# Edge pass of a graph network: operands of the one-hots and values moved to a PSUM bank, and an order of its own for TensorE

## The chip, the cores and the metric

The kernel runs on one core of a Trainium2 chip. The metric is the device time of one execution in microseconds, as the median of several executions. The engines are named as the profile names them: PE is TensorE (PEld is its weight load), DVE is VectorE, ACT is ScalarE, POOL is GpSimd and SP is SyncE.

## The reference, cut to what matters

A two-layer graph attention network over 6250 nodes and 100000 edges, followed by a feed-forward block on half of the rows. Everything that the change touches is the attention over edges, done once in each of the two layers:

```
src = concatenate([src0, arange(n)])        # self edges are added
dst = concatenate([dst0, arange(n)])        # dst0 comes sorted
q, k, v = ...reshape(n, 8, 32)              # 8 heads of 32
scores = einsum('ehd,ehd->eh', q[dst], k[src]) * scale
m   = segment_max(scores, dst)
ex  = exp(scores - m[dst])
z   = segment_sum(ex, dst)
agg = segment_sum((ex / z[dst])[:, :, None] * v[src], dst)
```

The two layers differ in weights only. Before, between and after them come dense stages over the nodes (projections, a merge of partial sums, normalisations, the feed-forward blocks), which the change leaves as they are.

## The kernel before, in words

`edge_pass` does the attention over edges of one layer. The sorted edges are cut into 832 steps of at most 128 edges with one block of 128 destination nodes each; eight steps are a group (`G = 8`), worked as four pairs (`PAIRS`, numbered `m` from 0 to 3). There are 104 groups in a pass. `groups_of` runs the first four and the last four groups as straight code and the others in a loop whose body holds four groups. A group's number modulo 4 is its lane; the buffers of rows `kv` have four lanes.

Five engines run one program each, tied by three counters (`dve_p`, `act_p`, `pe_p`: semaphores on which an engine ticks named steps, and on which the others wait for a step of a given group).

For each step, POOL gathers the key and value rows of the source nodes, 128 rows of 512 numbers, by an indirect DMA (L673) whose row numbers lie in the tile `idx` in SBUF. It waits until PE has ended its sums over the group that used the same lane four groups earlier. SP loads the small tables and the edges' offsets ahead.

DVE makes a one-hot matrix `spread` for a whole group from the offsets (L697). PE multiplies it with the block's queries, which gives each edge its query (`spread_q`, L805, step `q{m}`, two banks of PSUM, so two pairs ahead). DVE multiplies keys and queries (`product`, L715) and sums over each head (`score`, L722). When all four pairs of a group are done, PE transposes the scores into PSUM (`turn`, L834, step `score_t`), DVE takes the running maximum in both directions along the edges (`up`, L737, and `top`, L744), and PE transposes the maxima back (L842, step `max_t`). DVE subtracts them from the scores (`below`, L749) and keeps the maxima with the rows (`maxima`, L750), and ACT takes the exponential, which gives the weights (step `weights`, L909), into the columns `KV:KV + H` of `kv` in SBUF.

For each pair DVE then compares the column numbers 0 to 127 (`keep["cols"]`, a constant in SBUF) with each edge's node column (`tab`, SBUF), which gives a one-hot matrix (`sel`, L758), and multiplies the values by the weights in place (`value`, L764). PE multiplies the one-hots with the weighted values and adds into one of four PSUM banks (L852, steps `sums{j}`, two per pair); after two pairs it makes the sums of the rows at the ends of the steps (L863, steps `ends0` and `ends1`). ACT copies each step's sum bank to the accumulator `acc` (L919) and sets a bank that is done with to zero by copying a tile of zeros (L920, step `acc{j}`). PE's sums of a pair wait for ACT's `acc` of the step before it.

Both transposes share one bank of PSUM, `turned`: the scores turned are its first 128 columns on 64 partitions (`pst`), the maxima turned back are the 64 columns after them (`psm`).

The work of neighbouring groups is interleaved by a list, `WEAVE`, that DVE and PE both run through for each group; ACT has its own list, `ACT_WEAVE`. `product`, `score` and `turn` belong to the group itself. `up`, `top`, `weigh` (below and maxima) and `tail` (sel, value, sums of pairs 0 and 1) belong to the group before it, and `late` (the same of pairs 2 and 3) to the group two before it. An engine runs its instructions in the order of its program, so a wait holds up all that stands behind it. On PE `product m` stands for the `spread_q` two pairs ahead, that is of pair `m + 2` of the group or of pair `m - 2` of the next one.

Of the kernel before, what the change touches and what calls it, by code (L numbers as in the profile page):

```python
# [16 lines left out]
ALU = mybir.AluOpType  # L17
ACT = mybir.ActivationFunctionType
# [5 lines left out]
P = 128  # L24
N, D = 6250, 256
E = 100000
H, DH = 8, 32
# [3 lines left out]
SCALE = DH ** -0.5  # L31
# [13 lines left out]
G = 8  # L45
# [10 lines left out]
KV = 2 * D  # L56
# [93 lines left out]
def bc(ap, shape):  # L150

    return ap.broadcast_to(shape)
# [271 lines left out]
def constants(nc, keep):  # L424

    with Phase(nc) as ctx:
# [17 lines left out]
        def _(dve):  # L444
# [8 lines left out]

WEAVE = (("product", 0), ("late", 2), ("score", 0), ("up", 0), ("product", 1), ("top", 0), ("late", 3),
         ("score", 1), ("weigh", 0), ("product", 2), ("tail", 0), ("score", 2), ("product", 3), ("tail", 1),
         ("score", 3), ("turn", 0))
ACT_WEAVE = (("late", 2), ("weigh", 0), ("late", 3), ("tail", 0), ("tail", 1))
PAIRS = G // 2
# [5 lines left out]
def later(turn, n):  # L464

    lane, k, c = turn
    g = 4 * c + lane + n
    return (g % 4, k, g // 4)
# [5 lines left out]

CLEARED = 3

# [10 lines left out]
def edge_pass(nc, layer, dram, keep):  # L487

    with Phase(nc) as ctx:
# [3 lines left out]
        def ps(name, shape, dt=F32):  # L493
            return ctx.enter_context(nc.psum_tensor(f"edge{layer}_{name}", shape, dt))
# [5 lines left out]
        kv = sb("kv", [P, LANES, G, ROW])  # L500
# [11 lines left out]
        sel = sb("sel", [P, G, P])  # L512
        score = sb("score", [P, 2, G * H])
        up = sb("up", [G * H, P])
# [4 lines left out]
        pst = turned[0:G * H, 0:P]  # L519
        psm = turned[:, P:P + G * H]  # L520
        psa = ps("sums", [P, SUMS * BANKED])
        pse = ps("end_sums", [P, 512])
# [13 lines left out]
        for m in range(PAIRS):  # L536
            dve_steps += [f"product{m}", f"score{m}"]
        dve_steps += ["up", "top", "below", "maxima"]
        for m in range(PAIRS):
            dve_steps += [f"sel{m}", f"value{m}"]  # L540
        dve_p.begin(dve_steps)
        pe_p.begin([f"q{m}" for m in range(PAIRS)] + ["score_t", "max_t"] 
                   + [f"sums{j}" for j in range(HALF)] + ["ends0"] + [f"sums{j}" for j in range(HALF, G)] + ["ends1"])
# [142 lines left out]
        def _(dve):  # L686
            v = nc.vector
            v.memset(zeros[:, :], 0.0).then_inc(s_clear, 1)
            v.memset(blank[:, :], 0.0).then_inc(s_clear, 1)
            v.memset(pse[:, :], 0.0).then_inc(s_clear, 1)  # L690
            dve.wait_ge(s_clear, CLEARED)

# [38 lines left out]
            def scan_up(turn):  # L731
# [6 lines left out]
                           turn, "up")  # L738

            def rest(turn, what, m, earliest=False):  # L740
                lane = turn[0] % 2
                if what == "top":
                    dve_p.wait(dve, turn, "up")
                    dve_p.tick(v.tensor_tensor_scan(top[:, ::-1], flags[:, lane, 1, ::-1], up[:, ::-1], -BIG,  # L744
                                                    ALU.add, ALU.max), turn, "top")
                elif what == "weigh":
                    table(turn)
                    pe_p.wait(dve, turn, "max_t")
                    dve_p.tick(v.tensor_tensor(below[:, :], score[:, lane, :], psm, ALU.subtract), turn, "below")  # L749
                    dve_p.tick(v.tensor_tensor(kv[:, turn[0], :, KV + H:ROW], psm.rearrange("p (j h) -> p j h", h=H),  # L750
                                               bc(tab[:, turn[0], :, 1:2], [P, G, H]), ALU.mult),
                               turn, "maxima")
                elif what in ("tail", "late"):

                    if not earliest:
                        pe_p.wait(dve, later(turn, -1), f"sums{2 * m + 1}")
                    at = 2 * m
                    dve_p.tick(v.tensor_tensor(sel[:, at:at + 2, :], bc(keep["cols"][:, :].unsqueeze(1), [P, 2, P]),  # L758
                                               bc(tab[:, turn[0], 2 * m:2 * m + 2, 0:1], [P, 2, P]),
                                               ALU.is_equal), turn, f"sel{m}")  # L760
                    if m == 0:
                        act_p.wait(dve, turn, "weights")
                    values = kv[:, turn[0], 2 * m:2 * m + 2, D:KV].rearrange("p j (h d) -> p j h d", h=H)
                    dve_p.tick(v.tensor_tensor(values, values,  # L764
                                               bc(kv[:, turn[0], 2 * m:2 * m + 2, KV:KV + H].unsqueeze(3), [P, 2, H, DH]),
                                               ALU.mult), turn, f"value{m}")

            spread_of((0, None, 0), True)
            groups_of(dve, body)
            rest(later(LAST_TURN, -1), "late", 2)  # L770
            scan_up(LAST_TURN)
            rest(LAST_TURN, "top", 0)
# [6 lines left out]
        def _(pe):  # L779
# [36 lines left out]
            def body(turn, begun=4, end=False):  # L816
                places = {}
                for what, m in WEAVE:

# [60 lines left out]
        def _(act):  # L880
# [20 lines left out]
            def rest(turn, what, m, places, earliest=False):  # L901
                lane = turn[0] % 2
                if what == "weigh":
# [4 lines left out]
                    dve_p.wait(act, turn, "below")  # L908
                    act_p.tick(s.activation(kv[:, turn[0], :, KV:KV + H], below[:, :].rearrange("p (j h) -> p j h", h=H),  # L909
                                            ACT.Exp, scale=SCALE), turn, "weights")  # L910
                elif what in ("tail", "late"):
# [1550 lines left out]
```

## Time and profile before

| | us |
|---|---|
| median of 3 runs | 4388.59 (4388.18 to 4395.11) |
| the profiled execution, its time | 4386.98 |
| its span from the first to the last instruction | 4385.3 |
| busy: PE, DVE, ACT, POOL over the span | 3657.6, 3202.1, 1681.7, 2061.5 |

The time of the profiled execution is what the chip reported for it, and the span is what its trace shows between the first and the last instruction. In a row of a group of instructions, `x` is the count, then come busy microseconds and the mean nanoseconds of one, then the time that the engine sat idle just before them and what ended it (`<-`). "issue" is time in which the engine waited for nothing that the trace shows. In a row of the timeline the first two numbers are the start and the duration in microseconds, and the idle time just before stands in brackets.

### The profile page before, as it was taken

The page shows a single profiled execution, that of the slowest core. Times are in us where ns is not written, and L with a number is a line of the kernel's source. Part 1 is how long each engine was busy: PE and PEld are TensorE (multiplying, and loading weights), DVE is VectorE, ACT ScalarE, POOL GpSimd, SP SyncE. Part 2 cuts the span into 40 slices and gives each one's busy share as a digit, 9 for nine tenths or more (in the row PEclk, how much of TensorE's full clock was granted, in tenths as well). Part 3 has the DMA queues.
Part 4 walks back from the last instruction along what each step waited for, and adds up shares of the span by engine and source line. Part 5 has one row for each costly group of instructions (what it writes and reads, how often), then busy time and mean ns, then how long its engine had stood idle before and what let it go on. Part 6 is the DMA issues. An engine that isn't in the chain of part 4 may idle for free. (4 is left out here: it accounts for less than half of the span.)

```text
span 4385.3 us, 82262 instructions
## 1 busy us (share of the span) xinstructions
PE 3657.6 (83%) x17048; PEld 2421.9 (55%) x17048; DVE 3202.1 (73%) x7179; ACT 1681.7 (38%) x4755; POOL 2061.5 (47%) x1914
## 2 busy tenths in 40 slices
PE   1998889888898848999978898888889668888488
PEld 0654555555555427777755555555555337777377
DVE  4888999898989865555558898988899656666501
ACT  0114555555555502222225555555555302222022
POOL 2117777777777610000037777777777400000012
PEclk8999999999999979999989999999999879999699
DMA  3337777777777511111137777777777502222011
GB/s 72 120 112 220 217 217 220 212 216 211 215 215 218 173 62 48 48 60 60 48 118 211 214 219 211 218 213 209 212 219 220 165 22 75 84 78 78 26 46 39
DMA packets 357833, 640.42 MB, mean 146 GB/s; under 512 B 107755, under 2 KB 199981, under 8 KB 357594
## 3 DMA queue, kind: packets, MB, share of 16 engines
q0 software_dynamic: 140144, 457.44, 35.3%
q1 hardware_dynamic: 217610, 182.03, 14.1%
q8 instruction: 36, 0.59, 0.1%
q14 instruction: 43, 0.35, 0.0%
HBM read 570.14 MB, written 69.95 MB: 146 GB/s over the span
## 5 line engine op out<-in xcount | busy, mean ns | idle before, releaser
L673 POOL DMA_INDIRECT edge_kv<-kv,edge_idx x1664 | 1868.8, 1123 | 541.4 <-issue 416.9
L852 PE MATMUL edge_sums<-edge_kv,edge_sel 128*128 128x272 f32 x3328 | 982.9, 418 | 141.3 <-ACT edge_sums L920 111.8
L805 PE MATMUL edge_q<-qc,edge_spread 128*128 x3328 | 921.1, 400 | 153.1 <-DVE edge_kv L715 128.8
L919 ACT COPY acc<-edge_sums x1664 | 641.2, 385 | 869.5 <-PE edge_sums L852 699.2
L805 PEld LDWEIGHTS edge_q<-qc,edge_spread 128*128 128x128 f32 x3328 | 578.5, 191 | 431.6 <-issue 377.0
L852 PEld LDWEIGHTS edge_sums<-edge_kv,edge_sel 128*128 128x128 f32 x3328 | 567.5, 190 | 440.9 <-issue 363.1
L715 DVE TENSOR_TENSOR edge_kv<-edge_kv,edge_q 128x512 f32<-128x512 f32 x832 | 565.6, 680 | 242.9 <-DMA edge_kv<-kv,edge_idx 229.6
L920 ACT COPY edge_sums<-edge_blank 128x272 f32 x1664 | 659.7, 396 | 0.0
L764 DVE TENSOR_TENSOR edge_kv<-edge_kv 128x512 f32<-128x512 f32 x832 | 565.0, 679 | 0.8 <-ACT edge_kv L909 0.8
L722 DVE TENSOR_REDUCE edge_score<-edge_kv 128x16 f32<-128x512 f32 x832 | 560.0, 673 | 0.2
L758 DVE TENSOR_TENSOR edge_sel<-cols,edge_tab 128x256 f32<-128x256 f32 x832 | 340.3, 409 | 0.0
L1440 POOL TENSOR_TENSOR middle_rs<-middle_var,middle_power 128x2 f32<-128x2 f32 x50 | 34.7, 693 | 571.9 <-DVE middle_minus_half L1464 571.9
L863 PE MATMUL edge_end_sums<-edge_kv,edge_tab 128*2 128x272 f32 x3328 | 268.2, 394 | 0.0
L1440 POOL TENSOR_TENSOR last_rs<-last_var,last_power 128x2 f32<-128x2 f32 x50 | 34.7, 694 | 479.9 <-DVE last_minus_half L1464 479.9
L1627 PE MATMUL middle_ph<-middle_xt,middle_w 128*128 128x256 f32 x800 | 185.6, 386 | 28.5 <-ACT middle_xt L1705 28.5
L1627 PE MATMUL last_ph<-last_xt,last_w 128*128 128x256 f32 x800 | 181.7, 386 | 27.8 <-ACT last_xt L1705 27.8
L1627 PEld LDWEIGHTS last_ph<-last_xt,last_w 128*128 128x128 f32 x800 | 151.6, 192 | 53.9 <-ACT last_xt L1705 33.9
L1627 PEld LDWEIGHTS middle_ph<-middle_xt,middle_w 128*128 128x128 f32 x800 | 149.7, 192 | 53.4 <-ACT middle_xt L1705 20.4
L1637 PE MATMUL last_pp<-last_w,last_hid 128*128 128x256 f32 x800 | 176.7, 379 | 0.0
L1637 PE MATMUL middle_pp<-middle_w,middle_hid 128*128 128x256 f32 x800 | 176.7, 379 | 0.0
L697 DVE TENSOR_SCALAR edge_spread<-edge_rel,part 128x1024 f32<-128x1024 bf16 x208 | 160.3, 771 | 6.2 <-DMA edge_rel<-step_rel 6.2
L1637 PEld LDWEIGHTS last_pp<-last_w,last_hid 128*128 128x128 f32 x800 | 152.0, 190 | 20.7
(369 smaller groups left out, 3912.1 us busy)
## 6 DMA issues: line engine op xcount, KB each, us to landing
edge_rel<-step_rel SPq DMA_DIRECT2D x208, 256.0 KB
edge_kv<-kv,edge_idx POOLq DMA_INDIRECT x1664, 3.9
edge_flags<-step_flags SPq DMA_DIRECT2D x416, 32.0 KB
picked<-last_picked SPq DMA_DIRECT2D x25, 513.0 KB
kv<-first_kv_out SPq DMA_DIRECT2D x25, 512.0 KB
kv<-middle_kv_out SPq DMA_DIRECT2D x25, 512.0 KB
end_rows<-edge_ends SPq DMA_DIRECT2D x416, 8.5 KB
h<-first_h SPq DMA_DIRECT2D x25, 256.0 KB
```

The costliest lines, as they stand in the source:

```text
L673: nc.gpsimd.indirect_dma_start(kv[:, turn[0], j, 0:KV], None, dram["kv"], bass.IndirectOffsetOnAxis(ap=idx[:, turn[0], j:j + 1], axis=0)). ...
L715: dve_p.tick(v.tensor_tensor(k_rows, k_rows, psq[m % QBUFS][:, :, :], ALU.mult), turn, f"product{m}")
L722: dve_p.tick(v.tensor_reduce(score[:, lane, 2 * m * H:2 * (m + 1) * H].rearrange("p (j h) -> p j h", h=H), k_rows.rearrange("p j (h d) -> ...
L758: dve_p.tick(v.tensor_tensor(sel[:, at:at + 2, :], bc(keep["cols"][:, :].unsqueeze(1), [P, 2, P]), bc(tab[:, turn[0], 2 * m:2 * m + 2, 0:1 ...
L764: dve_p.tick(v.tensor_tensor(values, values, bc(kv[:, turn[0], 2 * m:2 * m + 2, KV:KV + H].unsqueeze(3), [P, 2, H, DH]), ALU.mult), turn, ...
L805: mm = t.matmul(psq[m % QBUFS][:, j % 2, :], spread[:, turn[0] % 2, j * P:(j + 1) * P], qc[:, bass.ds(at[j % 2], D)], start=True, stop=True)
L852: pe_p.tick(t.matmul(psa[:, bass.ds(place[j % 2], QC)], sel[:, j, :], kv[:, turn[0], j, D:ROW], start=False, stop=True, skip_group_check=T ...
L863: mm = t.matmul(pse[32 * q:32 * q + 2, 0:QC], tab[:, turn[0], j, 2:4], kv[:, turn[0], j, D:ROW], start=True, stop=True)
L919: s.copy(acc[:, bass.ds(at, QC)], psa[:, bass.ds(bank, QC)])
L920: act_p.tick(s.copy(psa[:, bass.ds(spent, QC)], blank[:, :]), turn, f"acc{j}")
L1627: mm = t.matmul(ph[bank // 2][:, at:at + W * P], mat[:, half, c * P:(c + 1) * P], xt[:, i, half * W * P:(half + 1) * W * P], start=(half = ...
L1637: mm = t.matmul(pp[turn[0]][:, w * D:(w + 1) * D], hid[:, turn[0], at:at + P], mat[:, c, :], start=(c == 0), stop=(c == FF // P - 1))
```

## The change

The column numbers are copied once per pass into the last 128 columns of the bank `turned` (`cols`), and `sel` reads them from there. The exponential is taken twice by ACT: into 64 more columns of that bank (`psw`), from which `value` now reads the weights, and as before into `kv`, with which PE sums them. `below` comes after `maxima`. DVE waits for the step `max_t` of the next group ahead of `late` 3 (`follows`), and for the weights ahead of the `sel` of pair 0, no longer between it and its `value`. `up` and `top` keep their place after `score` 0 and `product` 1 on DVE, while `late` 2 moves behind `up`, `late` 3 behind `product` 2, `weigh` behind `late` 3, and `tail` 0 behind `product` 3. PE gets its own list, `PE_WEAVE`, in which the transposes stand ahead of sums that they followed before: `max_t` directly behind `late` 2 and ahead of the `spread_q` of `product` 1, and the transpose of the scores ahead of the sums of `tail` 1. `late` 3 comes after the `spread_q` of `product` 2.

```diff
@@ -451,9 +451,11 @@
 
 
 
-WEAVE = (("product", 0), ("late", 2), ("score", 0), ("up", 0), ("product", 1), ("top", 0), ("late", 3),
-         ("score", 1), ("weigh", 0), ("product", 2), ("tail", 0), ("score", 2), ("product", 3), ("tail", 1),
+WEAVE = (("product", 0), ("score", 0), ("up", 0), ("late", 2), ("product", 1), ("top", 0), ("score", 1),
+         ("product", 2), ("late", 3), ("weigh", 0), ("score", 2), ("product", 3), ("tail", 0), ("tail", 1),
          ("score", 3), ("turn", 0))
+PE_WEAVE = (("product", 0), ("late", 2), ("top", 0), ("product", 1), ("product", 2), ("late", 3), ("product", 3),
+            ("tail", 0), ("turn", 0), ("tail", 1))
 ACT_WEAVE = (("late", 2), ("weigh", 0), ("late", 3), ("tail", 0), ("tail", 1))
 PAIRS = G // 2
 QBUFS = 2
@@ -472,7 +474,7 @@
     return turn[1] is None and turn[0] == 0 and turn[2] == 0
 
 
-CLEARED = 3
+CLEARED = 4
 
 
 def values_of(nc, engine, ap, most):
@@ -518,6 +520,8 @@
         turned = ps("turned", [P, 512])
         pst = turned[0:G * H, 0:P]
         psm = turned[:, P:P + G * H]
+        psw = turned[:, P + G * H:P + 2 * G * H].rearrange("p (j h) -> p j h", h=H)
+        cols = turned[:, 512 - P:512]
         psa = ps("sums", [P, SUMS * BANKED])
         pse = ps("end_sums", [P, 512])
 
@@ -535,11 +539,11 @@
         dve_steps = ["spread"]
         for m in range(PAIRS):
             dve_steps += [f"product{m}", f"score{m}"]
-        dve_steps += ["up", "top", "below", "maxima"]
+        dve_steps += ["up", "top", "maxima", "below"]
         for m in range(PAIRS):
             dve_steps += [f"sel{m}", f"value{m}"]
         dve_p.begin(dve_steps)
-        pe_p.begin([f"q{m}" for m in range(PAIRS)] + ["score_t", "max_t"] 
+        pe_p.begin([f"q{m}" for m in range(PAIRS)] + ["score_t", "max_t"]
                    + [f"sums{j}" for j in range(HALF)] + ["ends0"] + [f"sums{j}" for j in range(HALF, G)] + ["ends1"])
         act_p.begin(["weights"] + [f"acc{j}" for j in range(HALF)] + ["ends0"]
                     + [f"acc{j}" for j in range(HALF, G)] + ["ends1"])
@@ -688,6 +692,7 @@
             v.memset(zeros[:, :], 0.0).then_inc(s_clear, 1)
             v.memset(blank[:, :], 0.0).then_inc(s_clear, 1)
             v.memset(pse[:, :], 0.0).then_inc(s_clear, 1)
+            v.tensor_copy(cols, keep["cols"][:, :]).then_inc(s_clear, 1)
             dve.wait_ge(s_clear, CLEARED)
 
             def spread_of(turn, first=False):
@@ -737,6 +742,11 @@
                 dve_p.tick(v.tensor_tensor_scan(up[:, :], flags[:, lane % 2, 0, :], pst, -BIG, ALU.add, ALU.max),
                            turn, "up")
 
+            def follows(turn):
+
+                if turn[1] is not None or turn != LAST_TURN:
+                    pe_p.wait(dve, later(turn, 1), "max_t")
+
             def rest(turn, what, m, earliest=False):
                 lane = turn[0] % 2
                 if what == "top":
@@ -746,29 +756,31 @@
                 elif what == "weigh":
                     table(turn)
                     pe_p.wait(dve, turn, "max_t")
-                    dve_p.tick(v.tensor_tensor(below[:, :], score[:, lane, :], psm, ALU.subtract), turn, "below")
                     dve_p.tick(v.tensor_tensor(kv[:, turn[0], :, KV + H:ROW], psm.rearrange("p (j h) -> p j h", h=H),
                                                bc(tab[:, turn[0], :, 1:2], [P, G, H]), ALU.mult),
                                turn, "maxima")
+                    dve_p.tick(v.tensor_tensor(below[:, :], score[:, lane, :], psm, ALU.subtract), turn, "below")
                 elif what in ("tail", "late"):
 
                     if not earliest:
                         pe_p.wait(dve, later(turn, -1), f"sums{2 * m + 1}")
+                    if m == PAIRS - 1:
+                        follows(turn)
+                    if m == 0:
+                        act_p.wait(dve, turn, "weights")
                     at = 2 * m
-                    dve_p.tick(v.tensor_tensor(sel[:, at:at + 2, :], bc(keep["cols"][:, :].unsqueeze(1), [P, 2, P]),
+                    dve_p.tick(v.tensor_tensor(sel[:, at:at + 2, :], bc(cols.unsqueeze(1), [P, 2, P]),
                                                bc(tab[:, turn[0], 2 * m:2 * m + 2, 0:1], [P, 2, P]),
                                                ALU.is_equal), turn, f"sel{m}")
-                    if m == 0:
-                        act_p.wait(dve, turn, "weights")
                     values = kv[:, turn[0], 2 * m:2 * m + 2, D:KV].rearrange("p j (h d) -> p j h d", h=H)
                     dve_p.tick(v.tensor_tensor(values, values,
-                                               bc(kv[:, turn[0], 2 * m:2 * m + 2, KV:KV + H].unsqueeze(3), [P, 2, H, DH]),
+                                               bc(psw[:, 2 * m:2 * m + 2, :].unsqueeze(3), [P, 2, H, DH]),
                                                ALU.mult), turn, f"value{m}")
 
             spread_of((0, None, 0), True)
             groups_of(dve, body)
+            scan_up(LAST_TURN)
             rest(later(LAST_TURN, -1), "late", 2)
-            scan_up(LAST_TURN)
             rest(LAST_TURN, "top", 0)
             rest(later(LAST_TURN, -1), "late", 3)
             rest(LAST_TURN, "weigh", 0)
@@ -815,7 +827,7 @@
 
             def body(turn, begun=4, end=False):
                 places = {}
-                for what, m in WEAVE:
+                for what, m in PE_WEAVE:
 
                     owner, pair = (turn, m + QBUFS) if m + QBUFS < PAIRS else (later(turn, 1), m + QBUFS - PAIRS)
                     ahead, next_pair = (turn, pair + 1) if owner == turn and pair + 1 < PAIRS else \
@@ -906,8 +918,9 @@
                     wait_beside(act, s_clear, s_table[lane_], value if k is None else k * 64 + value)
                     places[0] = columns_at(turn, 0)
                     dve_p.wait(act, turn, "below")
-                    act_p.tick(s.activation(kv[:, turn[0], :, KV:KV + H], below[:, :].rearrange("p (j h) -> p j h", h=H),
-                                            ACT.Exp, scale=SCALE), turn, "weights")
+                    less = below[:, :].rearrange("p (j h) -> p j h", h=H)
+                    s.activation(psw, less, ACT.Exp, scale=SCALE)
+                    act_p.tick(s.activation(kv[:, turn[0], :, KV:KV + H], less, ACT.Exp, scale=SCALE), turn, "weights")
                 elif what in ("tail", "late"):
                     for j in (2 * m, 2 * m + 1):
                         place = places[0] if j == 0 and 0 in places else columns_at(turn, j)
```

## Rows read from the trace of the kernel before

**Rows 1.** The page: span, and busy time of each engine.
```profile
span 4385.3 us, 82262 instructions
...
PE 3657.6 (83%) x17048; PEld 2421.9 (55%) x17048; DVE 3202.1 (73%) x7179; ACT 1681.7 (38%) x4755; POOL 2061.5 (47%) x1914
```
**Rows 2.** One line, first and second pass: durations min/median/max in ns, first and last start.
```profile
L697 DVE TENSOR_SCALAR edge_spread<-edge_rel,part x104: 735/748/975, 328.9 to 1495.9; 128x1024 f32<-128x1024 bf16 x104
...
L697 DVE TENSOR_SCALAR edge_spread<-edge_rel,part x104: 735/748/985, 2261.8 to 3432.9; 128x1024 f32<-128x1024 bf16 x104
```
**Rows 3.** Busy time by stretch (PE, PEld, DVE, ACT, POOL; clock, DMA share, GB/s): 500 to 1500.
```profile
500.00:1500.00 1000.00, 889.45 (x4382) 516.36 (x4383) 903.81 (x1841) 552.98 (x1667) 786.40 (x702) 1.00 0.74 216
```
**Rows 4.** Groups of instructions in the stretch from 500 to 1500.
```profile
L673 POOL DMA_INDIRECT edge_kv<-kv,edge_idx x702 | 787.8, 1122 | 213.9 <-issue 174.9 <-PE edge_sums L852 23.1 <-PE edge_end_sums L863 15.8
...
L715 DVE TENSOR_TENSOR edge_kv<-edge_kv,edge_q 128x512 f32<-128x512 f32 x351 | 238.7, 680 | 92.9 <-DMA edge_kv<-kv,edge_idx 89.1 <-PE edge_q L805 2.3
L764 DVE TENSOR_TENSOR edge_kv<-edge_kv 128x512 f32<-128x512 f32 x351 | 238.4, 679 | 0.0
...
L722 DVE TENSOR_REDUCE edge_score<-edge_kv 128x16 f32<-128x512 f32 x350 | 235.6, 673 | 0.0
L758 DVE TENSOR_TENSOR edge_sel<-cols,edge_tab 128x256 f32<-128x256 f32 x351 | 143.5, 409 | 0.0
...
L737 DVE TENSOR_TENSOR_SCAN edge_up<-edge_flags,edge_turned 64x128 f32<-64x128 f32 x88 | 35.3, 401 | 0.5 <-PE edge_turned L834 0.4
...
L909 ACT ACTIVATE edge_kv<-edge_below 128x64 f32<-128x64 f32 x87 | 22.3, 257 | 80.8 <-DVE edge_below L749 80.0
```
**Rows 5.** One line, the gathers in that stretch: durations min/median/max in ns.
```profile
L673 POOL DMA_INDIRECT edge_kv<-kv,edge_idx x702: 942/946/2491, 499.3 to 1499.1; - x176
```
**Rows 6.** Timeline, 909 to 914: gathers, and what DVE runs meanwhile.
```profile
909.82 0.41 DVE L758 TENSOR_TENSOR edge_sel<-cols,edge_tab 128x256 f32<-128x256 f32 x1
909.83 1.82 POOL L673 DMA_INDIRECT edge_kv<-kv,edge_idx  x1 [0.30 <-issue]
...
910.15 0.68 DVE L764 TENSOR_TENSOR edge_kv<-edge_kv 128x512 f32<-128x512 f32 x1
...
911.95 0.74 DVE L697 TENSOR_SCALAR edge_spread<-edge_rel,part 128x1024 f32<-128x1024 bf16 x1
911.96 2.48 POOL L673 DMA_INDIRECT edge_kv<-kv,edge_idx  x1 [0.30 <-issue]
...
912.94 0.68 DVE L764 TENSOR_TENSOR edge_kv<-edge_kv 128x512 f32<-128x512 f32 x1
```
**Rows 7.** Timeline, one gather beside a product, from DVE's and POOL's own timelines.
```profile
895.75 0.68 DVE L715 TENSOR_TENSOR edge_kv<-edge_kv,edge_q 128x512 f32<-128x512 f32 x1
...
895.92 0.95 POOL L673 DMA_INDIRECT edge_kv<-kv,edge_idx  x1 [0.30 <-issue]
```
**Rows 8.** Timeline, 911 to 918: PE's order, and ACT's clearing that releases its sums.
```profile
911.99 1.18 PE L852 MATMUL edge_sums<-edge_kv,edge_sel 128*128 128x272 f32 x4 [0.59 <-ACT edge_sums L920]
...
913.10 0.64 PE L863 MATMUL edge_end_sums<-edge_kv,edge_tab 128*2 128x272 f32 x8
...
913.67 0.30 PE L834 MATMUL edge_turned<-ident,edge_score 128*64 128x128 f32 x1
...
913.81 1.03 PE L805 MATMUL edge_q<-qc,edge_spread 128*128 x4
...
914.00 0.40 ACT L920 COPY edge_sums<-edge_blank 128x272 f32 x1
...
914.67 1.14 PE L852 MATMUL edge_sums<-edge_kv,edge_sel 128*128 128x272 f32 x4
...
915.65 1.03 PE L805 MATMUL edge_q<-qc,edge_spread 128*128 x4
...
916.61 0.27 PE L842 MATMUL edge_turned<-ident,edge_top 64*128 64x64 f32 x1
917.27 1.18 PE L852 MATMUL edge_sums<-edge_kv,edge_sel 128*128 128x272 f32 x4 [0.39 <-ACT edge_sums L920]
```

## The prediction, made before the change was run

> **What bounds the kernel now.** I read the page first: no engine is busy for the whole span, PE comes nearest with 83% [rows 1]. Such shares mix stages, so next I looked for the edge passes by the one line that runs once a group, the making of `spread`. Its 104 starts per pass reach over 1167.0 us and 1171.1 us, so the 206 steps from one group to the next take 11.33 and 11.37 us, 11.35 in the mean, and the two passes hold 53% of the span [rows 2].
>
> Then the groups of instructions in a stretch inside the first pass. It holds 351 products, four to a group, thus 87.75 groups in 1000 us, 11.40 us each [rows 4]. Per group PE is busy 10.14 us, DVE 10.30, ACT 6.30 and POOL 8.96 [rows 3]. POOL looks idle, but before each of its 702 gathers stand 213.9 us in all, 0.305 us each, nearly all with no releaser. With the mean of 1.122 us a gather comes every 1.427 us, and eight of them every 11.41 us: the pace of the group. POOL is the bound, though its busy share does not say so. DVE bears it out: of its 96 us of idle time, 89.1 are waits of a product for gathered rows [rows 4].
>
> The reader is to see next that a gather needs no 1.122 us. The median is 0.946 and the longest 2.491 [rows 5]. What makes one long shows in the timeline. One starts 10 ns after a `sel`; `sel` and the `value` behind it end at 910.83, and the gather ends 0.82 us later, having taken 1.82. Another starts with `spread`, is held through `sel` and `value` to 913.62, and ends 0.82 us after that, having taken 2.48 [rows 6]. But one that starts inside a product takes 0.95 [rows 7]. `spread` reads in a form of its own; `sel` and `value` have two tensor inputs in SBUF; the product has one in SBUF and one in PSUM. So POOL is held by DVE instructions with two inputs in SBUF, and not by one whose second input is in PSUM.
>
> **The change part by part.** *Operands of `sel` and `value`.* Both get one input in PSUM, as the product has, so eight of DVE's instructions per group should cease to hold POOL. Left are `spread` and `top`. A gather's least cost is 0.946 + 0.305 = 1.25 us, eight are 10.0. A gather starts inside `spread` (0.748 us) in 0.748 / 1.25 = 0.6 of the groups and then loses on average a quarter of a microsecond; `top`, of the size of `up` (0.40), adds less. I take 10.2 us per group for POOL, with 10.0 and 11.41 (nothing freed) as bounds.
>
> *DVE's own time.* No row shows `sel` or `value` with a PSUM input. The nearest is the product of the same 128x512 shape: 680 ns with a PSUM input, 679 for `value` without one [rows 4]. I take no difference. The bound above is one read per two clocks where a weight is read 32 times over, costed under the rivals. The bound below is nothing: `value`, which meets POOL, is no longer than the product, which does not, so there is no wait in it to lose.
> The Trainium skill, Perfetto Trace Analysis (Optimizing Scalar/DVE Operations), speaks against this: about 60 ns of access for DVE on SBUF, about 125 on PSUM. By it, eight instructions would cost 0.52 us more per group, DVE would need 10.82 and set the pace, and the time would be 4278. The two rows above (680 and 679) do not show the rule.
>
> *The second exponential.* 208 times 0.257 us on ACT [rows 4], 53 us that its idle 45% hides. It also delays the weights by its 0.26, and `maxima` ahead of `below` by less than the 0.40 of `up`, which has twice the columns: at most 0.66. The wait for the weights now stands ahead of `sel` 0; behind it on DVE are both tails and the last score, and PE waits for all of these. But between `below` and `sel` 0 lie a score and a product, about 1.2 us, which cover both. Without that cover it would cost up to 0.66 us per group.
>
> *The copy of the columns*: once per pass, between `up`'s 0.40 us for 128 elements and nothing; 0.3 us each, 0.6 in all.
>
> *The wait `follows`.* DVE now waits for `max_t` ahead of `late` 3 instead of ahead of `below`. Queued behind it are `sel` and `value` 3, `weigh`, and the last two products; PE's sums and ACT's weights wait for those. Between `top` and this wait lie `score` 1 and `product` 2, about 1.2 us. `max_t` stands on PE behind the sums of `late` 2, and those behind ACT. So the question is how fast PE and ACT go round.
>
> *PE's new order.* Sums of one pair wait for ACT to have cleared behind the pair before. From one start of sums to the next it took 2.60 us (914.67 to 917.27, with PE idle 0.39 for ACT at its end) and 2.68 (911.99 to 914.67, filled by PE's own work) [rows 8]. PE's own pitches there are: sums to ends 1.11, ends 0.57, score transpose 0.14, `spread_q` 0.86 to 0.96, sums to `spread_q` 0.98, `max_t` 0.27. The old order puts at most 2.68 between neighbouring sums, so four rounds are some 10.5 us, under POOL's 11.4. In the new order:
> `late` 2 to `late` 3: sums 0.98, `max_t` 0.27, two `spread_q` 0.91 + 0.86 = 3.02, now PE's own work and longer than ACT's 2.60.
> `late` 3 to `tail` 0: 1.11 + 0.57 + 0.86 = 2.54, so ACT's 2.60.
> `tail` 0 to `tail` 1: 0.98 + 0.14, so 2.60. The score transpose sits in time in which PE waits anyway.
> `tail` 1 to the next `late` 2: 1.11 + 0.57 + 0.86 = 2.54, so 2.60.
> Sum 10.82. With `max_t` costing only 0.2 and all `spread_q` 0.86 it is 10.65. I take 10.75, and 10.5 to 11.0 as its own bounds.
>
> *Sum.* Per group POOL 10.2, DVE 10.30, PE with ACT 10.75; the last sets the pace, and DVE's 0.45 us of slack shows as waits for `max_t`. The gain is 206 x (11.35 - 10.75) = 124 us. The profiled execution took 4386.98 us (1.7 more than its span), 1.6 under the median; 4386.98 - 124 + 0.6 = 4264. The stages outside the edge passes keep their time.
>
> **The rivals.**
> *DVE sets the pace.* If PE and ACT go round quicker than my pitches say, DVE's 10.30 us is the limit: 206 x 1.05 = 216 us, 4171. For it: single pitches as short as 0.86, PE busy only 10.14 us per group. Against it: 2.60 between sums is ACT's, not PE's.
> *The new waits eat most of it.* Each late `max_t` stops DVE, which makes `value` 3 late and with it PE's next sums, and these the next `max_t`; three engines within 0.6 us of each other seldom all run at their limits. For it: PE already waits 0.39 and 0.59 us for ACT ahead of sums [rows 8]. Against it: the queries are made two pairs ahead, which leaves DVE work. At 11.0 us per group the time is 4315, at 11.3 it is 4377.
> *No change.* POOL is held by `spread` and by something other than the operands of `sel` and `value`. Then the gathers keep their mean of 1.122 us, eight keep 11.41, and the time stays near 4387. For it: the longest gathers do start at a `spread`. Against it: one starts at a `sel` and is held to the end of `value` [rows 6], and one beside a product is not held [rows 7].
> The Trainium skill, SBUF — State Buffer (Who interferes with whom), infers that a `tensor_tensor` takes only the read side of the port that DVE shares with GpSimd, while writing descriptors needs the write side, so that it would not stall a gather. The gather of 1.82 us beside `sel` and `value` says that here it does.
> *Slower: `value` reads the repeated weight from PSUM at half rate.* One element costs (679 - 409) / 256 = 1.05 ns by the rows of `value` and `sel` [rows 4]; doubled, each `value` takes 0.54 us more, four 2.16, DVE 12.46 per group, and the time is 4387 + 206 x 1.11 = 4616. It decides from 1.05 us per group, 0.26 per `value`. No row has a repeated read from PSUM; the product reads it straight, at full rate.
>
> **How the numbers follow.** PE with ACT at 10.5 to 11.0 us: 0.48 (4212 to 4315). DVE's pace, 10.2 to 10.5: 0.20. The new waits: 0.14. No change: 0.08. Slower: 0.10. The prediction is the first one's, 4264. 4140 to 4355 takes in nearly all of the first two and most of the third, about 0.79; both signs' other cases stay out. A measurement here can tell 0.2%, 9 us, from no change. Faster: 0.48 + 0.20 + 0.14 = 0.82; same 0.08; slower 0.10.
>
> **What would show it.** Gathers: their mean should fall from 1.122 to under 1.0 us, the long ones starting in `spread` or `top` alone; waits of products for gathered rows should nearly vanish, and POOL should wait for PE's sums instead. `sel` and `value` should keep 409 and 679 ns. DVE should wait for the transposed maxima at `sel` 3, some 0.4 us per group, and for nothing ahead of `sel` 0. Starts of `spread` should be 10.5 to 11.0 us apart. The prediction is wrong if the gathers stay long, if `value` grows, or if sums follow each other quicker than 2.6 us, as when ACT's clearing is not what they wait for.

## The result, and the profile after

The changed kernel takes 4446.40 us in the median of 4 runs (4441.65 to 4452.80) against 4388.39 of the kernel before: 1.0138 times as long, 95% interval 1.0108 to 1.0169. It is slower by 58 us where 124 us less were forecast.

The first rows are the page's span and busy times, then the line that makes `spread` in the first and the second pass (durations min/median/max in ns, first and last start in us), then the busy time in the stretch from 500 to 1500 us. They answer to [rows 1 to 3].

```profile
span 4440.0 us, 82786 instructions
...
PE 3621.0 (82%) x17048; PEld 2424.8 (55%) x17048; DVE 3196.4 (72%) x7181; ACT 1711.5 (39%) x4963; POOL 1798.8 (41%) x1914
```
```profile
L702 DVE TENSOR_SCALAR edge_spread<-edge_rel,part x104: 740/760/924, 331.6 to 1529.6; 128x1024 f32<-128x1024 bf16 x104
...
L702 DVE TENSOR_SCALAR edge_spread<-edge_rel,part x104: 744/778/869, 2295.5 to 3491.7; 128x1024 f32<-128x1024 bf16 x104
```
```profile
500.00:1500.00 1000.00, 851.05 (x4265) 501.60 (x4258) 875.04 (x1788) 549.28 (x1704) 656.15 (x682) 1.00 0.71 210
```

All of the loss is in the two passes. Over 103 steps they now take 1198.0 and 1196.2 us, 11.63 and 11.61 per group, in place of 1167.0 and 1171.1: together 56.1 us more, where the two profiled spans differ by 54.7. POOL lost 263 us of its busy time on the page, but no engine is busier in the pass: PE, DVE and POOL all do less per microsecond than before. That is the look of work held up by waits or by order.

The groups of instructions in the same stretch, then some of its waits (total, times, longest, in us), then the gathers alone (durations min/median/max in ns); the first rows answer to [rows 4], the last to [rows 5].

```profile
L677 POOL DMA_INDIRECT edge_kv<-kv,edge_idx x682 | 656.8, 963 | 344.2 <-issue 180.3 <-PE edge_end_sums L875 147.7 <-PE edge_sums L864 16.2
...
L720 DVE TENSOR_TENSOR edge_kv<-edge_kv,edge_q 128x512 f32<-128x512 f32 x341 | 231.1, 678 | 75.0 <-PE edge_q L817 64.4 <-issue 10.6
L776 DVE TENSOR_TENSOR edge_kv<-edge_kv,edge_turned 128x512 f32<-128x512 f32 x340 | 229.3, 674 | 0.0
...
L772 DVE TENSOR_TENSOR edge_sel<-edge_turned,edge_tab 128x256 f32<-128x256 f32 x340 | 139.9, 411 | 50.0 <-PE edge_turned L854 50.0
```
```profile
POOL edge_kv L677 <- PE edge_end_sums L875: 147.7, 81, 2.7
PE edge_sums L864 <- ACT edge_sums L933: 82.6, 64, 1.4
DVE edge_kv L720 <- PE edge_q L817: 64.4, 77, 1.3
...
DVE edge_sel L772 <- PE edge_turned L854: 50.0, 85, 0.8
```
```profile
L677 POOL DMA_INDIRECT edge_kv<-kv,edge_idx x682: 940/946/1174, 499.7 to 1499.4; - x171
```

The first half of the change did what it was to do. The gathers' mean fell from 1.122 to 0.963 us and their longest from 2.491 to 1.174; POOL now waits 147.7 us for PE's sums at the ends; and products no longer wait for gathered rows, a wait of 89.1 us before. But DVE is idle for longer than before, 125 us of the 1000 in place of 96, and now mostly for PE: 64.4 us for queries and 50.0 us for the transposed maxima. That points to PE as the new bound. One group of it, from PE's timeline:

```profile
906.98 1.08 PE L864 MATMUL edge_sums<-edge_kv,edge_sel 128*128 128x272 f32 x4
907.90 0.27 PE L846 MATMUL edge_turned<-ident,edge_score 128*64 128x128 f32 x1
909.43 1.18 PE L864 MATMUL edge_sums<-edge_kv,edge_sel 128*128 128x272 f32 x4 [1.26 <-ACT edge_sums L933]
910.54 0.64 PE L875 MATMUL edge_end_sums<-edge_kv,edge_tab 128*2 128x272 f32 x8
911.11 1.13 PE L817 MATMUL edge_q<-qc,edge_spread 128*128 x4
912.09 1.18 PE L864 MATMUL edge_sums<-edge_kv,edge_sel 128*128 128x272 f32 x4
913.20 0.27 PE L854 MATMUL edge_turned<-ident,edge_top 64*128 64x64 f32 x1
913.40 1.13 PE L817 MATMUL edge_q<-qc,edge_spread 128*128 x4
914.81 1.13 PE L817 MATMUL edge_q<-qc,edge_spread 128*128 x4 [0.28 <-issue]
915.77 1.15 PE L864 MATMUL edge_sums<-edge_kv,edge_sel 128*128 128x272 f32 x4
916.85 0.64 PE L875 MATMUL edge_end_sums<-edge_kv,edge_tab 128*2 128x272 f32 x8
917.42 1.13 PE L817 MATMUL edge_q<-qc,edge_spread 128*128 x4
918.39 0.94 PE L864 MATMUL edge_sums<-edge_kv,edge_sel 128*128 128x272 f32 x3
```

From sums to sums it goes 2.45 (`tail` 0 to `tail` 1, ended by ACT), 2.66, 3.68 (`late` 2 to `late` 3) and 2.62: 11.41 us. No wait for DVE stands in it. Averaged over 75 groups from 505 to 1395 us, the same four pieces take 2.54, 2.80, 3.78 and 2.64 us, 11.75 in all, so the group shown is one of the shorter ones. The wait ahead of the sums of `tail` 1 is 1.26 or 1.35 us in each of the 85 groups of the stretch. In 21 of them the profile names DVE's `sel` and not ACT, but there too ACT's clearing ended 0.24 us before the sums, as in the others of 1.35 us. In the long piece the two `spread_q` in a row come 1.41 us apart, though four matmuls in a row take less than 1. What PE's sequencer does between them shows in a view of the line that loads registers with addresses, for the stretch from 912 to 914.85 (the q marks the sequencer, whose instructions don't count as busy time; minimum, median and maximum in ns, first and last start in us):

```profile
L484 PEldq TENSOR_LOAD <-edge_regs_s x2: 541/542/543, 912.4 to 914.0; - x2
L484 PEldq TENSOR_LOAD <-edge_regs_q x1: 545/545/545, 913.4 to 913.4; - x1
```

Beside the four matmuls of 913.40 the sequencer loads the next query addresses (913.4, 0.545 us) and then the addresses of the sums of `tail` 0 (914.0, 0.54), and only after both does it send off the next `spread_q`. So theory 1 is that PE's own list sets the pace, and that two loads between two `spread_q` make its longest piece. Theory 2, the rival, is that DVE's new waits for PE set it (the maxima ahead of `late` 3, the queries of `product` 2). Theory 3 is that reading PSUM, or the second exponential, costs what was lost.

### The profile page after: what moved, and what is told of

It reads as the page before. It is cut to its first block and busy times, and to the rows that moved or that the text cites. A ratio compares the mean times of both kernels' runs of the same rounds, so it can differ in the third digit from the quotient of the medians.

```text
span 4440.0 us, 82786 instructions
## 1 busy us (share of the span) xinstructions
PE 3621.0 (82%) x17048; PEld 2424.8 (55%) x17048; DVE 3196.4 (72%) x7181; ACT 1711.5 (39%) x4963; POOL 1798.8 (41%) x1914
## 5 line engine op out<-in xcount | busy, mean ns | idle before, releaser
L677 POOL DMA_INDIRECT edge_kv<-kv,edge_idx x1664 | 1606.1, 965 | 835.3 <-issue 437.2
L864 PE MATMUL edge_sums<-edge_kv,edge_sel 128*128 128x272 f32 x3328 | 967.0, 413 | 284.2 <-ACT edge_sums L933 209.9
L817 PE MATMUL edge_q<-qc,edge_spread 128*128 x3328 | 947.3, 408 | 102.5 <-issue 72.1
L776 DVE TENSOR_TENSOR edge_kv<-edge_kv,edge_turned 128x512 f32<-128x512 f32 x832 | 561.1, 674 | 0.0
L772 DVE TENSOR_TENSOR edge_sel<-edge_turned,edge_tab 128x256 f32<-128x256 f32 x832 | 342.3, 411 | 126.8 <-PE edge_turned L854 125.7
```

The costliest lines, as they stand in the source:

```text
L677: nc.gpsimd.indirect_dma_start(kv[:, turn[0], j, 0:KV], None, dram["kv"], bass.IndirectOffsetOnAxis(ap=idx[:, turn[0], j:j + 1], axis=0)). ...
L772: dve_p.tick(v.tensor_tensor(sel[:, at:at + 2, :], bc(cols.unsqueeze(1), [P, 2, P]), bc(tab[:, turn[0], 2 * m:2 * m + 2, 0:1], [P, 2, P]), ...
L776: dve_p.tick(v.tensor_tensor(values, values, bc(psw[:, 2 * m:2 * m + 2, :].unsqueeze(3), [P, 2, H, DH]), ALU.mult), turn, f"value{m}")
L817: mm = t.matmul(psq[m % QBUFS][:, j % 2, :], spread[:, turn[0] % 2, j * P:(j + 1) * P], qc[:, bass.ds(at[j % 2], D)], start=True, stop=True)
L864: pe_p.tick(t.matmul(psa[:, bass.ds(place[j % 2], QC)], sel[:, j, :], kv[:, turn[0], j, D:ROW], start=False, stop=True, skip_group_check=T ...
```

## The experiments

All are edits of the changed kernel unless another is named. Pace is the distance of `spread`'s first and last start in the first pass over 103; the gathers' mean is over 500 to 1400 us. Each ratio is to the kernel before, run on the same chip.

| run | us | ratio (95%) | pace, us | gather, ns |
|---|---|---|---|---|
| e1_pe_as_dve | 4607.8 | 1.0501 (1.0480 to 1.0522) | 12.39 | 963 |
| e2_late3_first | 4228.75 | 0.9633 (0.9614 to 0.9652) | 10.61 | 984 |
| e3_sbuf_operands | 4444.62 | 1.0126 (1.0106 to 1.0145) | 11.65 | 1057 |
| e4_loads_ahead | 4516.62 | 1.0289 (1.0269 to 1.0309) | 11.97 | 955 |
| e5_late3_first_sbuf | 4329.34 | 0.9873 (0.9836 to 0.9910) | 11.06 | 1090 |
| e6_no_load | 4314.36 | 0.9837 (0.9800 to 0.9874) | 10.99 | 969 |
| e7_late3_first_sel_sbuf | 4234.04 | 0.9652 (0.9616 to 0.9689) | 10.63 | 990 |
| e8_late3_first_value_sbuf | 4240.05 | 0.9697 (0.9638 to 0.9755) | 10.61 | 1029 |
| e9_late3_first_no_load | 4248.02 | 0.9675 (0.9655 to 0.9695) | 10.70 | 980 |
| e10_before_no_load | 4395.59 | 1.0022 (1.0006 to 1.0038) | 11.37 | 1133 |

**e1_pe_as_dve**

```diff
-PE_WEAVE = (("product", 0), ("late", 2), ("top", 0), ...
+PE_WEAVE = WEAVE
```

> PE follows DVE's new order again; everything else is as in the changed kernel. Theory 1, PE's own list sets the pace of 11.75 us per group: between the sums of late 2 and late 3 stand then sums 1.1, one spread_q 0.97, the transpose of the maxima 0.2 and one spread_q 0.97, together 3.2 in place of 3.78; late 3 to tail 0 2.65, tail 0 to tail 1 2.55, tail 1 to late 2 2.8: 11.2 us per group, 206 x 0.55 = 113 us less than the changed kernel, about 4333. Theory 2, DVE's waits for the transposed maxima and for the queries of product 2 set the pace: the maxima come a spread_q later, DVE waits longer, and the time is 4446 or more.

161 us slower than the changed kernel. That is on theory 2's side, though not by the wait that it named. In the stretch from 500 to 1400 us DVE's `up` waits for the transposed scores:

```profile
L741 DVE TENSOR_TENSOR_SCAN edge_up<-edge_flags,edge_turned 64x128 f32<-64x128 f32 x72 | 29.7, 412 | 136.0 <-PE edge_turned L845 136.0
```

That is 1.89 us per group. In DVE's new order `up` comes right after `score` 0, with `late` 2 behind it, so a transpose that stands behind the sums of `tail` 1 and their ends is late, and with it everything on DVE. With DVE's new order, the transpose ahead of those sums is therefore a needed part of the change. My 11.2 us had left DVE out.

**e2_late3_first**

```diff
-... ("product", 1), ("product", 2), ("late", 3), ("product", 3), ("tail", 0), ("turn", 0), ("tail", 1))
+... ("product", 1), ("late", 3), ("product", 2), ("tail", 0), ("product", 3), ("turn", 0), ("tail", 1))
```

> Only PE's list is changed: the sums of late 3 stand directly behind the spread_q of product 1, the sums of tail 0 behind the spread_q of product 2, and the spread_q of product 3 between the sums of tail 0 and the transpose of the scores, so that no two spread_q stand in a row. Theory 1, PE's list sets the pace: late 2 to late 3 1.1 + 0.2 + 0.97 = 2.3, so ACT's 2.55; late 3 to tail 0 1.11 + 0.57 + 0.97 = 2.65; tail 0 to tail 1 0.96 + 0.97 + 0.14 = 2.1, so 2.55; tail 1 to late 2 2.65: 10.4 us per group, with DVE's 10.3 about 10.5, and 4446 - 206 x 1.25 = 4189. Theory 2, DVE's waits set it: the maxima and the queries of product 2 come where they came, so it stays near 4446.

218 us faster than the changed kernel and 160 us faster than the one before: it beats both. The same operands, the same orders on DVE and ACT, the same waits; only PE's list differs. PE's timeline:

```profile
906.85 1.18 PE L864 MATMUL edge_sums<-edge_kv,edge_sel 128*128 128x272 f32 x4 [0.19 <-DVE edge_kv L776]
907.95 0.64 PE L875 MATMUL edge_end_sums<-edge_kv,edge_tab 128*2 128x272 f32 x8
908.52 1.13 PE L817 MATMUL edge_q<-qc,edge_spread 128*128 x4
909.49 1.17 PE L864 MATMUL edge_sums<-edge_kv,edge_sel 128*128 128x272 f32 x4
910.50 1.03 PE L817 MATMUL edge_q<-qc,edge_spread 128*128 x4
911.36 0.27 PE L846 MATMUL edge_turned<-ident,edge_score 128*64 128x128 f32 x1
912.03 1.18 PE L864 MATMUL edge_sums<-edge_kv,edge_sel 128*128 128x272 f32 x4 [0.40 <-ACT edge_sums L933]
913.14 0.64 PE L875 MATMUL edge_end_sums<-edge_kv,edge_tab 128*2 128x272 f32 x8
913.71 1.13 PE L817 MATMUL edge_q<-qc,edge_spread 128*128 x4
914.68 1.08 PE L864 MATMUL edge_sums<-edge_kv,edge_sel 128*128 128x272 f32 x4
915.69 0.27 PE L854 MATMUL edge_turned<-ident,edge_top 64*128 64x64 f32 x1
915.89 1.13 PE L817 MATMUL edge_q<-qc,edge_spread 128*128 x4
917.31 0.95 PE L864 MATMUL edge_sums<-edge_kv,edge_sel 128*128 128x272 f32 x3 [0.29 <-DVE edge_kv L776]
```

The four pieces are 2.64, 2.54, 2.65 and 2.63. Each holds at most one `spread_q` in a row, and most of the time that PE spent waiting for ACT's clearing (1.26 us, now 0.40) or between two `spread_q` is now spent on matmuls. The short wait for `value` 3 (0.19 and 0.29 us) follows from DVE's wait for the maxima: `sel` 3 starts at 916.07, released by the transpose of 915.69, and `value` 3 behind it ends at 917.09.

**e3_sbuf_operands**

```diff
-            v.tensor_copy(cols, keep["cols"][:, :]).then_inc(s_clear, 1)
...
-bc(cols.unsqueeze(1), [P, 2, P])
+bc(keep["cols"][:, :].unsqueeze(1), [P, 2, P])
...
-bc(psw[:, 2 * m:2 * m + 2, :].unsqueeze(3), [P, 2, H, DH])
+bc(kv[:, turn[0], 2 * m:2 * m + 2, KV:KV + H].unsqueeze(3), [P, 2, H, DH])
...
-                    s.activation(psw, less, ACT.Exp, scale=SCALE)
```

> The new orders and waits stay, but sel and value read the column numbers and the weights from SBUF as before the change, and the second exponential is left away. Theory 1, PE's list sets the pace: the gathers go back to 1.12 us and eight of them to 11.4 us, still under PE's 11.75, so the time stays within 15 us of 4446 and the operands alone are worth nothing in this order. Theory 3, reading PSUM or the second exponential costs what was lost: the time falls to 4388 or below.

2 us from the changed kernel. Theory 3 falls, and the operands alone are worth nothing in this order. The gathers went back to 1.057 us and not, as expected, to 1.12. A likely reason, not tested by itself, is DVE's new order, which has `score` 0 behind `spread` where `sel` stood, so that fewer gathers collide.

**e4_loads_ahead**

```diff
+                        if m != 2:
+                            ahead_of(turn, m, places, begun)
...
+                        if m == 1:
+                            if not end:
+                                following = q_at(ahead, next_pair)
+                            ahead_of(turn, 2, places, begun)
                         spread_q(owner, pair, at)
...
```

> PE's register loads for the spread_q of product 2 and for the sums of tail 0 are made ahead of the spread_q of product 1, no longer between the two; the order of the matmuls stays. Theory 1 with the loads as cause of the 1.48 us between the two spread_q: they come 0.97 apart, late 2 to late 3 takes 3.3, the group 11.25 and the kernel 4446 - 206 x 0.5 = 4343; if the loads are only moved ahead of the first spread_q and are not hidden there, the pitch from the transpose to the first spread_q grows from 0.2 to 0.7 and the time stays. Theory 2, the second spread_q waits for product 2 on DVE: the pitch stays at 1.48.

70 us slower than the changed kernel. The loads went where they were put: PE's timeline shows the two `spread_q` as one run of eight matmuls, and the time now stands ahead of both.

```profile
907.06 0.27 PE L863 MATMUL edge_turned<-ident,edge_top 64*128 64x64 f32 x1
908.32 1.99 PE L817 MATMUL edge_q<-qc,edge_spread 128*128 x8 [0.99 <-issue]
```
```profile
L484 PEldq TENSOR_LOAD <-edge_regs_q x1: 546/546/546, 907.0 to 907.0; - x1
L484 PEldq TENSOR_LOAD <-edge_regs_s x1: 547/547/547, 907.6 to 907.6; - x1
```

The second `spread_q` did not wait for DVE. I had allowed for the loads being moved instead of hidden, but at 0.7 us; the pitch from the transpose to the first `spread_q` became 1.26, since the two loads that were moved now run one after the other beside and behind the transpose, from 907.0 to 908.2, before the first `spread_q` is sent off.

**e6_no_load**

```diff
+                    if k is not None or c > 0 or lane > 0:
+                        return 0, 0
                 return values_of(nc, "PE", regs_q[0:1, ...
```

> The changed kernel without PE's register load for the next group's first spread_q: the queries of each group's first pair are read from block 0 for all groups but the first, which leaves out that address. One of the two loads of 0.54 us that PE's sequencer makes between the spread_q of product 1 and that of product 2 is gone. Theory 1 with the loads as cause: the two come 0.97 to 1.0 apart in place of 1.48, the group takes 11.25 and the kernel 4446 - 206 x 0.5 = 4343. Rival, the second spread_q waits for DVE's product 2 or for the first one's bank: the pitch stays at 1.48 and the time at 4446.

132 us less than the changed kernel. With one of the two loads left out, the two `spread_q` run through without a gap, eight matmuls from 914.59 and the next sums at 916.54, 1.95 us for both:

```profile
914.59 2.11 PE L819 MATMUL edge_q<-qc,edge_spread 128*128 x8
916.54 1.11 PE L866 MATMUL edge_sums<-edge_kv,edge_sel 128*128 128x272 f32 x4
```

The gain is 29 us more than the half microsecond per group on which the expectation was built. Averaged over the groups from 505 to 1395 us, the piece from `late` 2 to `late` 3 fell by 0.61 us, from 3.78 to 3.16, and the sums behind it by 0.08, from 1.10 to 1.02; why those got shorter stays open.

**e9_late3_first_no_load and e10_before_no_load** leave out the same load, by the same two lines in `q_at`, in e2's list and in the kernel before.

```diff
+                    if k is not None or c > 0 or lane > 0:
+                        return 0, 0
```

> PE's list with late 3 first and the same load left out as in the changed kernel without it (each group's first pair reads its queries from block 0). Theory 1, a load of 0.54 us costs only where PE runs out of queued matmuls meanwhile: here it stands behind a spread_q whose 0.97 us and the wait for value 3 cover it, so the time stays within 15 us of 4229. Rival, PE's sequencer is itself the bound, and each load left out gives its 0.54 us per group: 4229 - 206 x 0.5 = 4125.

> The kernel before with the same load left out. By the prediction's reading, POOL sets the pace there, eight gathers of 1.427 us: within 0.3% of 4388. Rival, PE's list sets it there too: 4388 - 100.

No gain in either. e9 is 19 us above e2, which is 4 us outside what was expected. The waits from 500 to 1400 us, e2 first, show where:

```profile
PE edge_sums L864 <- DVE edge_kv L776: 19.2, 85, 0.3
```
```profile
PE edge_sums L866 <- DVE edge_kv L776: 26.7, 84, 0.4
```

PE's sums wait 0.32 us per group for `value` 3 in place of 0.23, and 206 x 0.09 is 19 us; why `value` 3 comes later stays open. So the load cost its time where PE had nothing queued to run meanwhile (e6) and nothing where matmuls and a wait covered it (e9); PE's sequencer as such is not the bound in e2's list. e10 is within 0.3% of the kernel before, as it must be if POOL set the pace there. By itself it doesn't show that, since a load that is covered would give nothing either.

**e5_late3_first_sbuf**: e2's list with the operands of e3, which leaves out the copy and the second exponential too.

```diff
+... ("product", 1), ("late", 3), ("product", 2), ("tail", 0), ("product", 3), ("turn", 0), ("tail", 1))
...
+bc(keep["cols"][:, :].unsqueeze(1), [P, 2, P])
...
+bc(kv[:, turn[0], 2 * m:2 * m + 2, KV:KV + H].unsqueeze(3), [P, 2, H, DH])
```

> PE's list with late 3 first, and sel and value reading SBUF as before the change. Theory 1, the operands free POOL, which counts once PE's list is quick enough: gathers go back to 1.12 us, eight with their 0.30 us between them to 11.4 us per group, and the time to about 4388 (4360 to 4420), 160 us above the same list with PSUM operands. Theory 4, PE's list alone made the gain: within 20 us of 4229.

101 us slower than e2: between the two theories, and it says that both halves count once PE is quick enough. DVE's products wait for gathered rows again, 63.6 us in 900:

```profile
POOL edge_kv L677 <- issue: 173.1, 568, 0.3
DVE edge_kv L719 <- DMA edge_kv<-kv,edge_idx: 63.6, 150, 1.0
...
POOL edge_kv L677 <- PE edge_sums L863: 15.8, 52, 0.3
POOL edge_kv L677 <- PE edge_end_sums L874: 7.9, 26, 0.3
```

POOL is the bound here: none of the 646 gaps ahead of its gathers is longer than 0.3 us, the gap that also stands where it waits for nothing. In the changed kernel they go up to 2.7. The time is 59 us under what I expected, since the gathers took 1.090 us and not 1.12, shorter than before the change with the same operands, as in e3.

**e7_late3_first_sel_sbuf and e8_late3_first_value_sbuf**: e2 with one of the two operands put back, the first diff for e7 (which also leaves out the copy) and the second for e8 (which leaves out the second exponential).

```diff
-bc(cols.unsqueeze(1), [P, 2, P])
+bc(keep["cols"][:, :].unsqueeze(1), [P, 2, P])
```
```diff
-bc(psw[:, 2 * m:2 * m + 2, :].unsqueeze(3), [P, 2, H, DH])
+bc(kv[:, turn[0], 2 * m:2 * m + 2, KV:KV + H].unsqueeze(3), [P, 2, H, DH])
```

> PE's list with late 3 first; value reads the weights from PSUM, sel the column numbers from SBUF. If a gather is held only to the end of the two-input instruction in which it starts, and one needs 0.82 us behind that end against 0.95 undisturbed: four sel of 0.41 us catch 1.3 starts per group and cost 0.1 us each, so the gathers' mean rises from 0.98 to 1.0 us and the time stays within 20 us of 4229. Rival, sel is what holds POOL: gathers near 1.1 us and a time over 4330.

> PE's list with late 3 first; sel reads the column numbers from PSUM, value the weights from SBUF, and the second exponential is left away. By the same reckoning four value of 0.68 us catch 2.2 starts per group and cost 0.22 us each, 0.5 us per group: gathers' mean 1.04 us, eight with their gaps 10.75 us, and a time of 4229 to 4270. Rival, value alone is what holds POOL: gathers near 1.1 us and a time over 4330.

Both as reckoned: 990 and 1029 ns, and a time within 12 us of e2. Either half of the operand change gets nearly all of the gain in time. The reckoning, which both runs fit, is that `sel` and `value` stand back to back: with both in SBUF, a gather that starts in `sel` is held through 1.0 us, with one of them only to that one's end. In e8 POOL is at its limit again (its longest gap is 0.3 us), at e2's pace.

## Why the prediction was wrong

*What bounds the kernel before* was right, but one of its readings proves nothing: the mean of a gather and of the idle time before it, times eight, is the pace of a group whatever sets it, since the two fill the stretch. What speaks for POOL is how long its gaps are, in the stretch from 500 to 1500 us of the kernel before:

```profile
POOL edge_kv L673 <- issue: 174.9, 574, 0.3
...
POOL edge_kv L673 <- PE edge_sums L852: 23.1, 76, 0.3
POOL edge_kv L673 <- PE edge_end_sums L863: 15.8, 52, 0.3
```

None is longer than 0.3 us, whoever is named, so nothing held POOL up for longer than the gap that stands ahead of every gather. And e5 is 101 us slower than e2 by giving the collisions back. The new operands in the old orders were not run.

*Operands of `sel` and `value`* was right in size. Gathers were to fall under 1.0 us and fell to 0.963. `sel` and `value` were to keep 409 and 679 ns and took 411 and 674, so the rival of a repeated read at half rate is out, and no surcharge for PSUM shows.
The Trainium skill, Perfetto Trace Analysis (Optimizing Scalar/DVE Operations), gives DVE about 60 ns of access on SBUF and about 125 ns on PSUM; these rows do not show the difference. The Trainium skill, SBUF — State Buffer (Who interferes with whom), has two statements: that a DVE instruction with two SBUF inputs contends with a GpSimd instruction that reads SBUF, and the inference that `tensor_tensor` does not stall descriptor generation. e2 against e5 (gathers of 984 and 1090 ns) agrees with the first and not with the second.

*The second exponential, the copy of the columns* cost nothing that can be seen (e3). *`follows`* shows nearly as forecast: 50.0 us over 85 groups, 0.59 each, where 0.4 was said. DVE's wait for queries, 64.4 us, was not forecast.

*PE's new order* is the step that failed, in one term: "`late` 2 to `late` 3: sums 0.98, `max_t` 0.27, two `spread_q` 0.91 + 0.86 = 3.02". It measured 3.68 in the group shown: sums 1.11, `max_t` 0.20, first `spread_q` 1.41, second 0.96; in the mean of 75 groups 3.78. The mechanism was right, that this piece is PE's own and the longest, and that PE with ACT sets the pace. The size was not. I took the pitch from one `spread_q` to the next from rows in which sums or a transpose follow, since the trace of before has no two in a row, and left out what PE's sequencer must do between them. The trace of before does hold those loads, 351 in the same stretch for the sums with a median of 544 ns, and I had not read the sequencer's rows. e6 (one load out) and e4 (loads moved) show that they are the cause, e2 that an order without the neighbourhood has the operands' gain.

The other three pieces were 2.62, 2.45 and 2.66 for my 2.60 each, so the sum of 10.82 became 11.41 in the group shown and 11.75 in the mean of the 75 groups (11.63 over the whole pass). Of those 0.93 us the long piece holds 0.76; `tail` 1 to `late` 2, at 2.80, holds 0.20, and why that one is longer I have not shown. The pace is above POOL's old 11.35, and so a gain turned into a loss. I had then taken 10.75 where my own table summed to 10.82, and a range for this term (10.5 to 11.0) that held the error of a tenth of a microsecond per matmul group, but no instruction that was missing from the table.

*The rivals*: none of them was it. "The new waits eat most of it" came nearest in the rows, since DVE does wait for PE, but those waits are not what makes the changed kernel slow: e2 keeps every wait in the program and gains 218 us. Of that rival's chain, e2's trace shows the last link, 0.23 us per group in which PE's sums wait for `value` 3.

## What to carry to other kernels

When an in-order engine's list is rewritten, price each neighbouring pair in the new list with what its sequencer does between them, register loads above all; a pitch read between other neighbours does not carry over. Freeing the engine that sets the pace is worth only the distance to the next one: here PE's ring in its new order lay above the old bound, and the operand change showed nothing (2 us) until PE's list was mended, and then 101 us. Two changes that arrive together are told apart by running each without the other. And an engine's busy time and idle time per group always add up to the pace, so they don't show what sets it; an engine whose idle time is never longer than a fixed gap does.

## What the runs showed of the hardware

The register loads of the edge pass, from a tile in SBUF, take 0.54 us on PE's sequencer for two numbers and 0.31 us on ACT's for four; what makes the difference stays open. On PE they hold back the matmuls behind them: two in a row between two groups of four matmuls put the second group 0.45 us later (1.41 in place of 0.96 us), and leaving out the same load where 0.97 us of matmuls and a wait cover it gave nothing back (e9).
The Trainium skill, DMA: Bandwidth & Descriptors (Latency and other measured facts), gives a floor of about 600 ns for `tensor_load`, without naming an engine. Both loads are under it here, PE's by a little and ACT's by half.

An indirect gather on POOL is held up by DVE's `tensor_tensor` if both inputs lie in SBUF and not if one lies in PSUM (gathers of up to 2.49 us before, up to 1.17 after). What it costs grows faster than the length of the holding run: taking away either half of a run of 1.0 us (e7, e8) left 990 and 1029 ns in the mean, while the whole run gave 1090 and its absence 984. That fits a gather that is held only if it starts inside the run.
